# Gated cross-attention block on one core: rows scaled a batch further ahead, and a transfer that feeds float32r transposes

## The chip, the cores and the metric

The kernel runs on one core of a Trainium2 chip. The metric is the device time of one execution in microseconds (us). The kernel before was timed three times (median 298.14 us); one further execution, taken by the hardware profiler, took 297.72 us, and its span (first to last instruction) is 295.9 us. Durations below are of that execution. The engines are PE (TensorE, with its weight loads listed as PEld), ACT (ScalarE), DVE (VectorE), POOL (GpSimd) and SP (SyncE, which here only issues transfers).

## The reference, cut to what matters

```python
def _L0_xattn_ref(query, memories, mask, W, b):
    q = jnp.einsum('bsd,od->bso', query, W) + b
    add_mask = (1.0 - mask.astype(q.dtype)) * NEG
    attn_logits = jnp.einsum('bqd,bkd->bqk', q, memories) + add_mask
    attn_weights = jax.nn.softmax(attn_logits, axis=-1)
    return jnp.einsum('bqk,bkd->bqd', attn_weights, memories)

def _L0_ffn_ref(x, weight):
    return jnp.einsum('bsi,oi->bso', x, jnp.sign(weight))

x = x + jnp.tanh(g_xattn[0]) * _L0_xattn_ref(_layernorm(x), ctx, mask, W, b)
x = x + jnp.tanh(g_ffn[0]) * _L0_ffn_ref(_layernorm(x), weight)
```

`x` is 64 batches of 256 rows by 256 columns, `ctx` 64 batches of 77 keys by 256, all float32; `W` and `weight` are 256 by 256.

## The kernel before

A batch of 256 rows lies in SBUF as 128 partitions with two rows each (`j` = 0, 1). The work is software-pipelined over batches. In slot t every engine works in a fixed, hand-written order on several batches at once: PE transposes the probabilities of batch t-1 (`pt_ps`, L619), in even slots transposes the keys of two later batches (`ctx_ps`, L560), forms the logits of batch t (`l_ps`, L636) interleaved with the transposes of the attention result of batch t-2 (`x1t_ps`, L642), applies the probabilities of batch t-1 to the keys (`pv_ps`, L655), does half of a product of keys and query weights (`ctx_ps`, L568), transposes the scaled rows of batch t+1 (`xt_ps`, L601: four 128 by 128 transposes in float32) and last the feed-forward product of batch t-2 (`ffn_ps`, L673: eight matmuls of 256 columns in float32r, with the input split in a high part `x1_hi` and a low part `x1_lo`). An even slot and the odd one after it have different work, so times repeat in pairs of slots. `pipeline` runs slots 0 to 7 and 56 to 66 written out and slots 8 to 55 in a loop of eight.

The scaled rows `xs` are x times 1/deviation plus a shift, both found by DVE (`moments`, L437) and POOL (L270 to L286). ACT makes them (`scale_rows`, L333), one instruction for each j. ACT's order in slot t is: p_t (L395), in even slots ctx_t (L346), ffn_scaled (L402), xs of batch t+2 with j = 0, x_hi (L409), prob (L414), m_sb (L352), x_t of batch t+1 (`transposed_x`, L378), xs of batch t+2 with j = 1. `xs` has two buffers.

DVE's order is: the moments of x1, the reciprocal, y (L507), c1 (L518, which waits for the logits in `l_ps`), the masked logits and their extremes (L521), x_lo (L529), x1 (L537), the moments of x (L437). POOL's is: 1/deviation and shift of batch t+3, the second half of y (L313, which waits for ffn_scaled), the second 1/deviation, c2 (L324), neg_mask (L278).

SP issues, slot by slot: the load of x for batch t+5, in even slots the keys and masks of batches t+4 and t+5, and the store of y of batch t-3, which waits for DVE's and POOL's half of y. PE waits for `lo_done` (x_lo) before its feed-forward matmuls, for `xt_done` (x_t) before the logits, and for `pt_done` (p_t) before `pv_ps`.

Of the kernel before, what the change touches and what calls it, by code (L numbers as in the profile page):

```python
# [5 lines left out]
F32 = mybir.dt.float32  # L6
F32R = mybir.dt.float32r
I32 = mybir.dt.int32
ALU = mybir.AluOpType
ACT = mybir.ActivationFunctionType  # L10
AX = mybir.AxisListType

P = 128
N = 8
R = 4
# [5 lines left out]
DMA = 16  # L21


def flamingo_block(nc: bass.Bass, x: bass.AP, ctx: bass.AP, mask: bass.AP, g_xattn: bass.AP,
# [14 lines left out]
    NB, S, D = x.shape  # L39
    K = ctx.shape[1]  # L40
    T = S // P
# [8 lines left out]
    with ExitStack() as stack:  # L50
        def sb(name, shape, dt=F32):
            return stack.enter_context(nc.sbuf_tensor(name, shape, dt))

        def ps(name, shape):
            return stack.enter_context(nc.psum_tensor(name, shape, F32))

        def sem(name):
            return stack.enter_context(nc.semaphore(name))


        ident = sb("ident", [P, P])
        wq_raw = sb("wq_raw", [P, C, D])
        wq_c = sb("wq_c", [P, C, D])
        wf_raw = sb("wf_raw", [P, C, D])
# [16 lines left out]
        x_in = sb("x_in", [P, N, T, D])  # L81
# [1 line left out]
        ctx_v = sb("ctx_v", [K, N, D])  # L83
        ctx_t = sb("ctx_t", [P, C, 2, K])
        m_sb = sb("m_sb", [P, C, R, K])
        xs = sb("xs", [P, 2, T, D])
        x_t = sb("x_t", [P, 2, C, S])
        neg_mask = sb("neg_mask", [P, 2, T, K])
        neg_l = sb("neg_l", [P, 2, T, K])
# [22 lines left out]
        xt_ps = ps("xt_ps", [P, C, S])  # L112
# [11 lines left out]
        wf_loaded = sem("wf_loaded")  # L124
        ident_ready = sem("ident_ready")
        half_ready = sem("half_ready")
        gate_ready = sem("gate_ready")
        tanh_ready = sem("tanh_ready")
        prep_step = sem("prep_step")
# [11 lines left out]
        mr1_done = sem("mr1_done")  # L141
        shift1_done = sem("shift1_done")
        xs_done = sem("xs_done")
        negmask_done = sem("negmask_done")
        xt_psum = sem("xt_psum")
        xt_done = sem("xt_done")
# [26 lines left out]
        def at_least(eng, s, value):  # L173

            if not isinstance(value, int) or value > 0:
                eng.wait_ge(s, value)

        def landed(t0, n, ring=N):

            return t0 * (DMA // ring) + DMA * (n // ring + 1)  # L180

        def exists(t0, n):

            return not isinstance(t0, int) or 0 <= t0 + n < NB

        FIRST = N
        LAST = NB - N
        END = NB + 3

        def pipeline(eng, slot, after={}):  # L190

# [7 lines left out]
            with eng.Fori(FIRST // N, LAST // N) as group:  # L199
                for r in range(N):  # L200
                    slot(group * N, r)
            for t in range(LAST, END):
                slot(t - t % N, t % N)
# [4 lines left out]
        @block.sync  # L208
        def _(sp):
            def load_x(t0, n):  # L210
                sp.dma_start(x_in[:, n % N], x_rows[t0 + n]).then_inc(x_loaded[n % N], DMA)

            def load_mask(t0, n):

                i = n % N
                sp.dma_start(mask_in[:, i:i + 2],
                             mask_pairs[:, bass.ds(t0 + n, 2)]).then_inc(mask_loaded[i // 2], DMA)

            def load_ctx(t0, n):

                i = n % N
                sp.dma_start(ctx_v[:, i:i + 2],
                             ctx_keys[:, bass.ds(t0 + n, 2)]).then_inc(ctx_loaded[i // 2], DMA)

            load_x(0, 0)
            load_ctx(0, 0)
            load_x(0, 1)
            load_mask(0, 0)
            load_x(0, 2)
            load_ctx(0, 2)  # L230
            load_x(0, 3)
            load_mask(0, 2)
            load_x(0, 4)

            def slot(t0, r):
                t = t0 + r
                if exists(t0, r + AHEAD):
                    at_least(sp, x1_done, t - 2)
                    load_x(t0, r + AHEAD)
                if r % 2 == 0 and exists(t0, r + 4):  # L240
                    at_least(sp, pv_psum, t - 2)
                    at_least(sp, negmask_done, t - 2)
                    load_ctx(t0, r + 4)
                    load_mask(t0, r + 4)
                if exists(t0, r - 3):
                    i = (r - 3) % R
                    at_least(sp, y_done, t - 2)
                    at_least(sp, y_last_done, t - 2)
                    sp.dma_start(out_rows[t - 3], y[:, i]).then_inc(y_stored[i], DMA)

            pipeline(sp, slot)
            for i in range(R):
                sp.wait_ge(y_stored[i], DMA * (NB // R))
# [78 lines left out]
        def _(act):  # L332
            def scale_rows(t0, n, j):  # L333

                if j == 0:
                    act.wait_ge(shift1_done, t0 + n + 1)
                    act.wait_ge(x_loaded[n % N], landed(t0, n))
                    at_least(act, xt_psum, t0 + n - 1)
                act.activation(xs[:, n % 2, j], x_in[:, n % N, j], ACT.Identity,  # L339
                               scale=rstd1[:, n % R, j:j + 1],  # L340
                               bias=shift1[:, n % R, j:j + 1]).then_inc(xs_done, 1)

# [47 lines left out]
            def slot(t0, r):  # L390
                t = t0 + r
                if exists(t0, r - 1):
                    act.wait_ge(pt_psum, t)
                    at_least(act, pv_psum, t - 2)
                    act.activation(p_t[:, (r - 1) % 2], pt_ps[0:K, 0:S], ACT.Copy).then_inc(pt_done, 1)  # L395
                if r % 2 == 0 and exists(t0, r + 2):
                    keys_step(2 * t + 5)
                if exists(t0, r - 3):
                    act.wait_ge(c2_done, t - 2)
                    act.wait_ge(ffn_psum, t - 2)  # L400
                    at_least(act, y_last_done, t - 4)
                    act.activation(ffn_scaled[:, (r - 3) % 2], ffn_ps[T - 1][:, 0:D], ACT.Copy,  # L402
                                   scale=c2[:, (r - 3) % R, T - 1:T]).then_inc(ffn_scaled_done, 1)
                if exists(t0, r + 2):
                    scale_rows(t0, r + 2, 0)
                if exists(t0, r - 2):
                    act.wait_ge(x1t_psum, t - 1)
                    at_least(act, ffn_psum, t - 3)
                    act.activation(x1_hi[:, r % 2], x1t_ps[:], ACT.Copy).then_inc(hi_done, 1)  # L409
                if exists(t0, r):  # L410
                    act.wait_ge(logits_done, t + 1)
                    at_least(act, pt_psum, t - 1)
                    for j in range(T):
                        ins = act.activation(prob[:, r % 2, j], neg_l[:, r % 2, j], ACT.Exp, scale=-1.0,  # L414
                                             bias=neg_max[:, r % R, j:j + 1],
                                             accum_out=prob_sum[:, r % R, j:j + 1])
                    ins.then_inc(exp_done, 1)
                if isinstance(t, int) and t == 0:
                    gates()
                if r % 2 == 0 and exists(t0, r + 2):  # L420
                    m_step(0, (r // 2 + 1) % 2, 2 * t + 6)
                if r % 2 == 1 and exists(t0, r + 1):
                    m_step(1, (r // 2 + 1) % 2, 2 * t + 6)
                if exists(t0, r + 1):
                    transposed_x(t0, r + 1)
                if exists(t0, r + 2):
                    scale_rows(t0, r + 2, 1)

            pipeline(act, slot, {1: ffn_weights})


        @block.vector
        def _(dve):
            def moments(src, st, i, k, done):


                dve.bn_stats(st[:, k].rearrange("p j s -> p (j s)"),  # L437
                             src[:, i].rearrange("p j d -> p d j")).then_inc(done, 1)

            def stats1(n):  # L440
                dve.wait_ge(x_loaded[n], DMA)
# [18 lines left out]
            for c in range(C):  # L460
                ins = dve.tensor_scalar(wq_c[:, c], wq_raw[:, c], row_mean[:, c:c + 1], None, ALU.subtract)
# [91 lines left out]
        def _(pe):  # L553
# [10 lines left out]
            def m_step(c, count):  # L564

                pe.wait_ge(ctx_done, count)
                for o in range(C):
                    ins = pe.matmul(ctx_ps[:, 0:2 * K], wq_c[:, o, c * P:(c + 1) * P],  # L568
                                    ctx_t[:, o].rearrange("p b k -> p (b k)"),
                                    start=(o == 0), stop=(o == C - 1))  # L570
                ins.then_inc(ctx_psum, c + 1)
# [22 lines left out]

            def transpose_x(t0, n):

                pe.wait_ge(xs_done, T * (t0 + n + 1))
                at_least(pe, xt_done, t0 + n)
                for c in range(C):
                    for j in range(T):  # L600
                        ins = pe.transpose(xt_ps[:, c, j * P:(j + 1) * P],  # L601
                                           xs[:, n % 2, j, c * P:(c + 1) * P], ident[:])
                ins.then_inc(xt_psum, 1)

            transpose_x(0, 0)
            m_step(1, 2)

            def pair_keys(t0, r):
                pe.wait_ge(ctx_loaded[(r + 2) % N // 2], landed(t0, r + 2))
# [91 lines left out]
```

## Time and profile before

| | |
|---|---|
| three timed runs | 297.14, 298.14, 298.19 us |
| profiled execution | 297.72 us, span 295.9 us |
| PE / PEld busy | 285.6 / 275.4 us (97% / 93% of the span) |
| ACT, DVE, POOL busy | 253.9, 250.6, 214.1 us |
| granted TensorE clock, mean | 0.996 of full |
| moved by DMA | 44.39 MB, mean 150 GB/s |

A timeline row gives start, length and count of neighbouring equal instructions. PE's matmuls are pipelined: the length of one includes its latency, and what a matmul costs the stream is the distance from its start to the start of the next. Likewise on ACT an instruction may start shortly before the end of the one before it.

### The profile page before, as it was taken

The numbers are of one execution on the slowest core, as the hardware profiler recorded it, in microseconds if no ns is written. First come the engines' busy times: TensorE is split into PE (matmuls) and PEld (weight loads), VectorE is DVE, ScalarE is ACT, GpSimd is POOL, SyncE is SP. The second block draws the span as 40 slices with busy tenths as digits, with TensorE's granted clock in tenths as the row PEclk, the third lists the DMA queues.
The fourth block names the chain that finished last, engine by engine and source line by source line (L and its number), as shares of the span: only waits on it lengthen the run. The fifth ranks groups of instructions, "written<-read, shape, count | busy, mean of one in ns | idle before, by whom it ended". The sixth has DMA issues, their size and how long they took to land.

```text
span 295.9 us, 9253 instructions
## 1 busy us (share of the span) xinstructions
PE 285.6 (97%) x2338; PEld 275.4 (93%) x2338; DVE 250.6 (85%) x785; ACT 253.9 (86%) x738; POOL 214.1 (72%) x585
## 2 busy tenths in 40 slices
PE   7799999999999999999999999999999999999982
PEld 6599999999999999999999999999999999999972
DVE  3578988988898898889889888988988898898883
ACT  2689999999999998999999999999989999999841
POOL 2667777778777777877777787777778777777543
PEclk9999999999999999999999999999999999999998
DMA  6933445554544555454445545544654544441112
GB/s 192 281 90 115 149 143 154 188 167 145 161 153 142 159 184 168 137 167 154 141 156 184 171 140 160 153 143 155 184 172 138 167 151 143 154 151 71 73 56 88
DMA packets 33538, 44.39 MB, mean 150 GB/s; under 512 B 3504, under 2 KB 17136, under 8 KB 33520
## 3 DMA queue, kind: packets, MB, share of 16 engines
q1 hardware_dynamic: 32416, 43.66, 46.3%
q10 hardware_dynamic: 1104, 0.53, 0.6%
q8 instruction: 7, 0.11, 0.1%
q14 instruction: 11, 0.09, 0.1%
HBM read 27.40 MB, written 16.78 MB: 149 GB/s over the span
## 4 chain that ended last, share of the span: by engine, by line
PE 91%; DMA 3%; POOL 2%; DVE 1%; issue 1%; ACT 1%; SPq 1%; POOLq 0%; ACTq 0%
PE ffn_ps L673 20%; PE pv_ps L655 18%; PE l_ps L636 16%; PE ctx_ps L568 11%; PE x1t_ps L642 9%; PE xt_ps L601 9%; PE pt_ps L619 5%; PE ctx_ps L560 3%; DMA x_in<-in_x_dram 3%; POOL rstd L275 1%; POOL y L313 0%; DVE x_lo L529 0%; DVE c L518 0%; ACT ffn_scaled L402 0%; POOLq L50 0%
## 5 line engine op out<-in xcount | busy, mean ns | idle before, releaser
L275 POOL TENSOR_TENSOR rstd<-ve,minus_half 128x2 f32<-128x2 f32 x128 | 89.0, 695 | 10.0
L636 PE MATMUL l_ps<-m_sb,x_t 128*128 128x77 f32 x512 | 78.8, 257 | 0.9 <-ACT m_sb L352 0.5
L636 PEld LDWEIGHTS l_ps<-m_sb,x_t 128*128 128x128 f32 x512 | 74.6, 191 | 1.4 <-ACT x_t L378 1.3
L339 ACT ACTIVATE xs<-x_in,shift,rstd 128x256 f32<-128x256 f32 x126 | 74.6, 593 | 1.0 <-POOL shift L286 1.0
L642 PE MATMUL x1t_ps<-ident,x 128*128 128x128 f32 x256 | 68.8, 273 | 0.0
L655 PE MATMUL pv_ps<-ctx_v,p_t 77*128 77x256 f32 x256 | 66.1, 380 | 0.0
L673 PE MATMUL ffn_ps<-wf_t,x_hi 128*128 128x256 f32 x256 | 56.5, 301 | 2.5 <-DVE x_lo L529 2.4
L537 DVE SCALAR_TENSOR_TENSOR x<-pv_ps,c,x_in 128x256 f32<-128x256 f32 x128 | 55.3, 472 | 0.0
L414 ACT ACTIVATE prob<-neg_l,neg_max 128x77 f32<-128x77 f32 x128 | 44.6, 351 | 10.1 <-DVE neg_max L521 10.1
L313 POOL TENSOR_TENSOR y<-ffn_scaled,x 128x256 f32<-128x256 f32 x64 | 46.3, 724 | 9.2 <-ACT ffn_scaled L402 9.2
L529 DVE TENSOR_TENSOR x_lo<-x1t_ps,x_hi 128x512 fp32r<-128x512 f32 x64 | 43.9, 686 | 9.6 <-ACT x_hi L409 9.6
L673 PE MATMUL ffn_ps<-wf_t,x_lo 128*128 128x256 f32 x256 | 51.2, 282 | 0.0
L437 DVE BATCH_NORM_STATS2 st<-x_in 128x6 f32<-128x512 f32 x64 | 45.0, 704 | 6.9 <-DMA x_in<-in_x_dram 6.9
L270 POOL TENSOR_TENSOR ve<-st,eps 128x2 f32<-128x2 f32 x128 | 24.6, 192 | 33.9 <-DVE st L437 31.5
L642 PEld LDWEIGHTS x1t_ps<-ident,x 128*128 128x128 f32 x256 | 47.2, 185 | 0.0
L655 PEld LDWEIGHTS pv_ps<-ctx_v,p_t 77*128 77x128 f32 x256 | 43.5, 190 | 3.8 <-ACT p_t L395 0.3
L518 DVE TENSOR_TENSOR c<-recip,gate_attn 128x2 f32<-128x2 f32 x64 | 25.9, 405 | 23.2 <-PE l_ps L636 19.5
L568 PE MATMUL ctx_ps<-ctx_t,wq_c 128*128 128x154 f32 x256 | 44.4, 294 | 0.5 <-ACT ctx_t L346 0.5
L568 PEld LDWEIGHTS ctx_ps<-ctx_t,wq_c 128*128 128x128 f32 x256 | 41.0, 190 | 4.0 <-ACT ctx_t L346 0.7
L437 DVE BATCH_NORM_STATS2 st<-x 128x6 f32<-128x512 f32 x64 | 44.0, 688 | 0.2
L673 PEld LDWEIGHTS ffn_ps<-wf_t,x_hi 128*128 128x128 f32 x256 | 38.9, 189 | 4.0 <-DVE x_lo L529 3.8
L378 ACT ACTIVATE x_t<-xt_ps 128x512 f32<-128x512 f32 x64 | 38.3, 598 | 2.6 <-PE xt_ps L601 0.2
(49 smaller groups left out, 477.8 us busy)
## 6 DMA issues: line engine op xcount, KB each, us to landing
x_in<-in_x_dram SPq DMA_DIRECT2D x64, 256.0 KB, 2.7
out_dram<-y SPq DMA_DIRECT2D x64, 256.0 KB, 2.1
ctx_v<-in_ctx_dram SPq DMA_DIRECT2D x32, 154.0 KB
mask_in<-in_mask_BxSxS_ik_dram SPq DMA_DIRECT2D x32, 154.0 KB, 3.1
wq_raw<-in_L_xattn_W_dram ACTq DMA_DIRECT2D x1, 256.0 KB, 4.2
wf_raw<-in_L_ffn_weight_dram ACTq DMA_DIRECT2D x1, 256.0 KB, 5.6
bq_col<-in_L_xattn_b_dram ACTq DMA_DIRECT2D x1, 1.0 KB, 4.5
g_raw<-in_g_xattn_dram ACTq DMA_DIRECT2D x1, 0.5 KB, 6.2
```

The source lines that it names most:

```text
L275: pool.tensor_tensor(res[:, i], ve[:, i], minus_half[:], ALU.pow).then_inc(res_done, 1)
L313: pool.tensor_tensor(y[:, i, T - 1], ffn_scaled[:, (r - 3) % 2], x1[:, i, T - 1], ALU.add).then_inc(y_last_done, 1)
L339: act.activation(xs[:, n % 2, j], x_in[:, n % N, j], ACT.Identity, scale=rstd1[:, n % R, j:j + 1], bias=shift1[:, n % R, j:j + 1]).then_in ...
L414: ins = act.activation(prob[:, r % 2, j], neg_l[:, r % 2, j], ACT.Exp, scale=-1.0, bias=neg_max[:, r % R, j:j + 1], accum_out=prob_sum[:, ...
L437: dve.bn_stats(st[:, k].rearrange("p j s -> p (j s)"), src[:, i].rearrange("p j d -> p d j")).then_inc(done, 1)
L529: dve.tensor_tensor(x1_lo[:, r % 2], x1t_ps[:], x1_hi[:, r % 2].bitcast(F32), ALU.subtract).then_inc(lo_done, 1)
L537: ins = dve.scalar_tensor_tensor(out=x1[:, i, j], in0=pv_ps[:, j], scalar=c1[:, i, j:j + 1], in1=x_in[:, (r - 1) % N, j], op0=ALU.mult, op ...
L568: ins = pe.matmul(ctx_ps[:, 0:2 * K], wq_c[:, o, c * P:(c + 1) * P], ctx_t[:, o].rearrange("p b k -> p (b k)"), start=(o == 0), stop=(o == ...
L636: ins = pe.matmul(l_ps[:, j * K:(j + 1) * K], x_t[:, r % 2, c, j * P:(j + 1) * P], m_sb[:, c, r % R], start=(c == 0), stop=(c == C - 1))
L642: ins = pe.transpose(x1t_ps[:, c, j * P:(j + 1) * P], x1[:, (r - 2) % R, j, c * P:(c + 1) * P], ident[:])
L655: ins = pe.matmul(pv_ps[:, j], p_t[:, (r - 1) % 2, j * P:(j + 1) * P], ctx_v[:, i], start=True, stop=True)
L673: ins = pe.matmul(ffn_ps[j][:, 0:D], part[:, r % 2, c, j * P:(j + 1) * P], wf_t[:, c], start=(n == 0 and c == 0), stop=(n == 1 and c == C ...
```

## The change

Four things change. `xs` gets four buffers, and ACT makes both halves of a batch's scaled rows at the end of slot t, for batch t+3; only in slot 0 are those of batch 2 still made at the old places. For batches 4 to 59, SP issues at the head of slot t a transfer within SBUF, of 256 KB, that copies the scaled rows of batch t+2 into a new float32r tile `xs_r` with two buffers (through a view as float32, so the bits are kept); it waits for these rows. PE waits for this transfer in place of the rows and transposes from `xs_r` with a float32r identity, into a view of `xt_ps` as float32r. DVE makes that identity once, at its start. Batches 0 to 3 and 60 to 63 are transposed as before.

```diff
+        ident_r = sb("ident_r", [P, P], F32R)
-        xs = sb("xs", [P, 2, T, D])
+        xs = sb("xs", [P, R, T, D])
+        xs_r = sb("xs_r", [P, 2, T, D], F32R)
...
+        def moves(t0, n):
+            return not isinstance(t0, int) or MOVE_FIRST <= t0 + n < MOVE_END
+        def moved(t0, n):
+            return t0 * (DMA // 2) + DMA * ((n - MOVE_FIRST) // 2 + 1)
...
+        MOVE_FIRST = 4
+        MOVE_END = NB - 4
...
+            def move_xs(t0, n):
+                i = n % 2
+                sp.wait_ge(xs_done, T * (t0 + n + 1))
+                sp.dma_start(xs_r[:, i].bitcast(F32), xs[:, n % R]).then_inc(xs_moved[i], DMA)
             def slot(t0, r):
                 t = t0 + r
+                if moves(t0, r + 2):
+                    move_xs(t0, r + 2)
                 if exists(t0, r + AHEAD):
...
-                    at_least(act, xt_psum, t0 + n - 1)
-                act.activation(xs[:, n % 2, j], x_in[:, n % N, j], ACT.Identity,
+                    at_least(act, xt_psum, t0 + n - 3)
+                act.activation(xs[:, n % R, j], x_in[:, n % N, j], ACT.Identity,
...
-                if exists(t0, r + 2):
+                if isinstance(t, int) and t == 0:
                     scale_rows(t0, r + 2, 0)
...
-                if exists(t0, r + 2):
+                if isinstance(t, int) and t == 0:
                     scale_rows(t0, r + 2, 1)
+                if exists(t0, r + 3):
+                    for j in range(T):
+                        scale_rows(t0, r + 3, j)
...
+            dve.wait_ge(ident_ready, 2)
+            dve.tensor_copy(ident_r[:], ident[:]).then_inc(ident_r_ready, 1)
...
-                pe.wait_ge(xs_done, T * (t0 + n + 1))
+                if moves(t0, n):
+                    pe.wait_ge(xs_moved[n % 2], moved(t0, n))
+                else:
+                    pe.wait_ge(xs_done, T * (t0 + n + 1))
                 at_least(pe, xt_done, t0 + n)
                 for c in range(C):
                     for j in range(T):
-                        ins = pe.transpose(xt_ps[:, c, j * P:(j + 1) * P],
-                                           xs[:, n % 2, j, c * P:(c + 1) * P], ident[:])
+                        if moves(t0, n):
+                            ins = pe.transpose(xt_ps[:, c, j * P:(j + 1) * P].bitcast(F32R),
+                                               xs_r[:, n % 2, j, c * P:(c + 1) * P], ident_r[:])
+                        else:
+                            ins = pe.transpose(xt_ps[:, c, j * P:(j + 1) * P],
+                                               xs[:, n % R, j, c * P:(c + 1) * P], ident[:])
                 ins.then_inc(xt_psum, 1)
             transpose_x(0, 0)
             m_step(1, 2)
+            pe.wait_ge(ident_r_ready, 1)
```

## Rows read from the trace of the kernel before

**Rows 1.** The page: busy time by engine, and the last chain by line.

```profile
PE 285.6 (97%) x2338; PEld 275.4 (93%) x2338; DVE 250.6 (85%) x785; ACT 253.9 (86%) x738; POOL 214.1 (72%) x585
...
PE ffn_ps L673 20%; PE pv_ps L655 18%; PE l_ps L636 16%; PE ctx_ps L568 11%; PE x1t_ps L642 9%; PE xt_ps L601 9%; PE pt_ps L619 5%; PE ctx_ps L560 3%; DMA x_in<-in_x_dram 3%; POOL rstd L275 1%; POOL y L313 0%; DVE x_lo L529 0%; DVE c L518 0%; ACT ffn_scaled L402 0%; POOLq L50 0%
```

**Rows 2.** Waits from 24 to 278 us: last row (total, times, longest, us).

```profile
ACT p_t L395 <- PE pt_ps L619: 1.0, 6, 0.2
```

**Rows 3.** Timeline of PE: even slot from 156.57, one row of an odd slot.

```profile
153.79 1.03 PE L655 MATMUL pv_ps<-ctx_v,p_t 77*128 77x256 f32 x4
...
156.33 0.40 PE L673 MATMUL ffn_ps<-wf_t,x_lo 128*128 128x256 f32 x2
156.57 0.38 PE L619 MATMUL pt_ps<-ident,prob 128*77 128x128 f32 x2
156.79 0.43 PE L560 MATMUL ctx_ps<-ident,ctx_v 77*128 77x77 f32 x4
157.06 0.39 PE L636 MATMUL l_ps<-m_sb,x_t 128*128 128x77 f32 x2
...
157.97 0.34 PE L636 MATMUL l_ps<-m_sb,x_t 128*128 128x77 f32 x2
158.15 0.27 PE L642 MATMUL x1t_ps<-ident,x 128*128 128x128 f32 x1
158.26 1.03 PE L655 MATMUL pv_ps<-ctx_v,p_t 77*128 77x256 f32 x4
159.12 0.69 PE L568 MATMUL ctx_ps<-ctx_t,wq_c 128*128 128x154 f32 x4
159.65 0.60 PE L601 MATMUL xt_ps<-ident,xs 128*128 128x128 f32 x4
```

**Rows 4.** Timeline of ACT, two slots: their x_t and what follows.

```profile
151.65 0.60 ACT L378 ACTIVATE x_t<-xt_ps 128x512 f32<-128x512 f32 x1
...
155.82 0.60 ACT L378 ACTIVATE x_t<-xt_ps 128x512 f32<-128x512 f32 x1
156.32 0.59 ACT L339 ACTIVATE xs<-x_in,shift,rstd 128x256 f32<-128x256 f32 x1
156.99 0.38 ACT L395 ACTIVATE p_t<-pt_ps 77x256 f32<-77x256 f32 x1
157.27 0.42 ACT L346 ACTIVATE ctx_t<-ctx_ps 128x308 f32<-128x308 f32 x1
157.58 0.47 ACT L402 ACTIVATE ffn_scaled<-ffn_ps,c 128x256 f32<-128x256 f32 x1
157.94 0.60 ACT L339 ACTIVATE xs<-x_in,shift,rstd 128x256 f32<-128x256 f32 x1
158.46 0.60 ACT L409 ACTIVATE x_hi<-x1t_ps 128x512 fp32r<-128x512 f32 x1
```

**Rows 5.** Timeline of DVE and POOL, odd slot's c, then the even slot.

```profile
153.89 0.16 DVE L518 TENSOR_TENSOR c<-recip,gate_attn 128x2 f32<-128x2 f32 x1
...
158.26 0.72 POOL L313 TENSOR_TENSOR y<-ffn_scaled,x 128x256 f32<-128x256 f32 x1
158.35 0.65 DVE L518 TENSOR_TENSOR c<-recip,gate_attn 128x2 f32<-128x2 f32 x1 [0.58 <-PE l_ps L636]
...
159.24 0.68 DVE L529 TENSOR_TENSOR x_lo<-x1t_ps,x_hi 128x512 fp32r<-128x512 f32 x1
```

**Rows 6.** Timeline of SP's queue; the page's DMA queue and issues.

```profile
155.74 0.33 SPq L211 DMA_DIRECT2D x_in<-in_x_dram  x1
...
q1 hardware_dynamic: 32416, 43.66, 46.3%
...
x_in<-in_x_dram SPq DMA_DIRECT2D x64, 256.0 KB, 2.7
```

**Rows 7.** Timeline of the fill: ACT, POOL and PE.

```profile
14.02 0.65 POOL L286 TENSOR_TENSOR shift<-one,mr 128x2 f32<-128x2 f32 x1
...
14.67 0.59 ACT L339 ACTIVATE xs<-x_in,shift,rstd 128x256 f32<-128x256 f32 x1
15.16 0.37 ACT L395 ACTIVATE p_t<-pt_ps 77x256 f32<-77x256 f32 x1
...
15.77 1.07 PE L655 MATMUL pv_ps<-ctx_v,p_t 77*128 77x256 f32 x4
```

More of the change, by code:

```diff
@@ L126, in flamingo_block @@
         half_ready = sem("half_ready")
+        ident_r_ready = sem("ident_r_ready")
         gate_ready = sem("gate_ready")
@@ L143, in flamingo_block @@
         xs_done = sem("xs_done")
+        xs_moved = [sem(f"xs_moved{i}") for i in range(2)]
         negmask_done = sem("negmask_done")
```

## The prediction

> **What bounds the kernel now.** First the page. PE is busy for 97% of the span, and the chain that ended last runs through PE's lines almost alone [rows 1]; the transposes that the change touches, xt_ps, are 9% of it. Next the waits of the steady part: no row has PE or PEld as the waiting engine, and the last of all rows is 1.0 us in total [rows 2]. So PE's own stream sets the pace. The distance between two pv_ps, 153.79 and 158.26, is 4.47 us [rows 3], that between two x_t, 151.65 and 155.82, is 4.17 us [rows 4]: the first holds the even slot's key transposes, the second doesn't, and the even slot runs from 156.57 to about 161.04. A time that is taken from that stream is gained, as long as the other engines' answers are in time.
>
> **The price of a transpose.** Per instruction the stream costs the distance between starts [rows 3]. Float32: the four pv_ps take from 158.26 to 159.12, 0.215 us each for 256 columns, 0.84 ns a column. The four xt_ps take (0.60-0.27)/3 = 0.109 us each for 128 columns, 0.85 ns a column, so they run at the float32 rate. Float32r: the two ffn_ps from 156.33 to 156.57 take 0.12 us each for 256 columns, 0.46 ns a column. No row has float32r with fewer than 256 columns, nor a float32r transpose, so its price has to be bounded. From below: 128 columns at 0.46 ns are 0.059 us, and the nearest row for a weight load of 128 columns is ctx_ps at 156.79, four in 0.27 us, 0.067 us each. From above: two l_ps and one x1t_ps start within 157.97 to 158.15; the first step is some 0.07 us, like the 77 columns of ctx_ps, so the second is 0.11 us although only 77 columns stream in it. There the load of x1, or the turn to a transpose, is the limit. A float32r pass is 0.12 us at worst like ffn_ps. Between 0.059 (everything at the float32r rate) and 0.109 (nothing gained) I take the middle, 0.084 us: the operand is still four bytes wide to load and to pass through, only the stream is known to be faster.
>
> So four transposes a batch save 4 x 0.025 = 0.10 us, and 56 batches (4 to 59) save **5.6 us**. With 0.067 it would be 4 x 0.042 x 56 = 9.4 us, with 0.12 a loss of 2.5 us.
>
> The Trainium skill, "TensorE: Matmul & The Clock Gate", section "LDWEIGHTS (loading the stationary operand)", has a rule against this change: a load takes its columns divided by 1.2 GHz, whatever the rows. By it 128 columns would take 107 ns and hide any faster stream. The four ctx_ps at 0.067 us have a stationary operand of 128 columns too, and do not agree; the 0.11 us before x1t_ps does.
>
> **Can the others follow?** Before ffn_ps PE waits for x_lo. In the even slot x_lo ends at 159.92 [rows 5], and the last xt_ps starts at 159.65+0.33 = 159.98 [rows 3], with the load of ffn_ps right behind: no room at all. What makes x_lo late is c, which waits for the logits until 158.35 and then takes 0.65 us where the odd slot's takes 0.16; it ends at 159.00, with POOL's y (158.26+0.72 = 158.98) [rows 5].
>
> The Trainium skill, "SBUF — State Buffer", says that VectorE with two SBUF inputs and GpSimd share a port pair as an exclusive lock, and that the loser waits for the whole instruction; the 0.65 against 0.16 us agrees.
>
> The change moves that y. ACT's order after x_t becomes xs, xs, p_t, ctx_t, ffn_scaled. By distances between starts [rows 4]: x_t 155.82, first xs at +0.50, second at +1.02 (157.94 to 158.46 is 0.52 for an xs), p_t at +1.54 = 157.36, ctx_t +0.28, ffn_scaled +0.31 = 157.95, end 158.42 instead of 158.05. POOL's y can begin only near 158.48. c begins at 158.35 and is done at 158.51, ahead of it. x_lo then waits for x_hi alone (158.46+0.60), runs 159.09 to 159.77 and gives PE 159.82 with the usual 0.05 us for a signal: 0.16 us of room against 0.10 that I need. In the odd slot the y of POOL does not meet c, and the room by the same chain is about as large. x_hi itself isn't late: ACT is free at 158.31 and x1t_ps ends at 158.42.
>
> p_t is the second answer. In the odd slot x_t starts at 151.65, so p_t starts at 153.19 and ends at 153.57, and pv_ps starts at 153.79 with its load some 0.1 us earlier. 0.1 us is left where there was 0.5; it hides the move at nothing, and if an xs took 0.1 us longer PE would wait in every odd slot. In the even slot p_t ends at 157.74 for 158.26. ctx_t isn't needed until 159.12.
>
> **The transfer.** xs of batch t+3 ends in this trace at 155.82+1.02+0.59 = 157.43. SP now waits for it, in front of the load of x which stood at 155.74, so that load and the keys and masks behind it go some 2.1 us later; x lands in 2.7 us [rows 6], near 160.6, and DVE takes its moments at the end of the slot that begins at 161.04, behind an x_lo that comes 2.67 us into a slot (159.24 less 156.57), so after 163.7. The copy issued at 157.5 has no row of its own kind; at 2.7 us it lands at 160.2, and PE wants it in the slot from 161.04, as far into it as the odd slot's xt_ps lie: x_t at 155.82 starts as they end, 4.47+4.17 us before its counterpart of two slots on, so they start near 163.9. So over 3 us cover it, and 0 is the price. It adds 56 x 0.262 = 14.7 MB; 43.66 MB took 46.3% of the engines, so 62% will be busy: still no bound. The stores behind these issues wait for y anyway. DVE's copy of the identity falls in its first wait for x. Between 0 and +0.5 us for all of this.
>
> **The fill.** Here the change costs. In slot 0 ACT has to make two more xs in front of p_t. The second xs of batch 2 starts at 14.67, shift of batch 3 is there at 14.02+0.65 = 14.67, so p_t starts at 14.67+0.49+2 x 0.52 = 16.2 instead of 15.16 and ends at 16.57; pv_ps goes from 15.77 to about 16.65, **+0.9 us** [rows 7]. In slot 1 the same two xs and two copies of the ffn weights stand before p_t, some 0.3 us more, of which a wait for the first x_lo gives back a part. I take +1.0 us, between +0.4 and +1.5. The drain has no xs and doesn't change.
>
> **Sum.** 297.7 - 5.6 + 1.0 = 293.1 us for an execution like the profiled one. That lies 0.4 us below the median of the timed runs, so the forecast is **293.5 us**; own range 291 to 296.
>
> **Rivals.**
> (a) The full rate: 0.067 us or less. PE would save up to 0.17 us a slot, but x_lo allows 0.16: 298.1 + 1.0 - 56 x 0.16 = 290.1 us. For it speak ctx_ps's steps; against it, the 0.11 before x1t_ps. Chance 0.16.
> (b) The load of the four-byte operand is the bound, 0.11 us: nothing saved, the fill is lost, 299.2 us with 0 to +2.5 more. The Trainium skill's load rule leads here. Chance 0.15, mostly within the error.
> (c) float32r in short streams costs what a full float32 matmul costs, which is two instructions of 0.84 ns a column: 0.215 us for 128 columns. +0.106 x 4 x 56 = +23.7 us, 323 us. Only the absence of any float32r below 256 columns speaks for it; the kernel does its 154-column product in float32. Chance 0.08.
> (d) Slower by order: POOL's y begins before c in the even slot. Then c is held until 158.48+0.72 = 159.20, x_lo ends 0.20 later than now and PE's ffn_ps start 0.19 late, in 28 even slots: +5.3 us, while only 28 odd slots save 0.10. 298.1+1.0+5.3-2.8 = 301.6 us. It decides at 0.1 us: whether ffn_scaled ends before the logits do. A late p_t in odd slots would have the same sign. Chance 0.08.
> (e) The copy or the later loads aren't in time and PE waits for DMA: no row comes nearer than 3 us. 298 to 302 us. Chance 0.03.
> Forecast: 0.50.
>
> **How the numbers follow.** A difference of 0.5% (1.5 us) is what can be told from none. Faster: forecast and (a) together, 0.66. Slower by more: (c), (d), half of (e) and a third of (b): 0.21. The rest, 0.13, is no change. The range goes down to (a) with an easier fill, 289, and up past (b) to 300.5; outside are (c), most of (d) and a little below: some 0.17.
>
> **What would show it.** Right: four xt_ps some 0.52 us long in place of 0.60, no wait of PE in the steady part, distances between pv_ps of 4.37 us; c in even slots back at 0.16 us; pv_ps of the fill near 16.6. Wrong: steps of 0.11 or 0.2 us within xt_ps; PEld waiting for x_lo or p_t; c still at 0.65.

## The result and the profile after

| | before | changed |
|---|---|---|
| median of 20 timed runs | 297.94 us | 295.23 us |
| profiled execution, span | 297.72, 295.9 us | 296.76, 295.0 us |
| medians of a second series | 297.53 us (30 runs) | 296.82 us (12 runs) |

The ratio of the changed kernel to the one before is 0.9928, with an interval of 0.9914 to 0.9942: faster by 0.7%. In the second series it is 0.9971 (0.9947 to 0.9995). The sign was forecast, and the size was not: 1.5% was expected. One execution of each kernel (472.8 and 551.8 us) was in a much slower state and is left out of the ratio and of the spreads that follow. The changed kernel also spreads more, from 294.6 to 297.8 us in its first 20 runs (297.1 to 298.6 before), and part of the answer lies in that.

The page of the changed kernel, the lines on engines, the DMA queue and the new transfer:

```profile
PE 284.4 (96%) x2338; PEld 273.9 (93%) x2338; DVE 242.0 (82%) x786; ACT 250.9 (85%) x738; POOL 215.6 (73%) x585
...
q1 hardware_dynamic: 40480, 58.34, 60.7%
...
xs_r<-xs SPq DMA_DIRECT2D x56, 256.0 KB, 2.3
```

PE still bounds the kernel [rows 1]. The copies brought the queue from 46.3% to 60.7% [rows 6] and land in 2.3 us.

The waits of the steady part, 24 to 276 us, of the changed kernel:

```profile
POOL ve L293 <- DVE st L463: 20.9, 46, 2.7
DVE c L547 <- PE l_ps L674: 18.8, 46, 0.8
DVE x_lo L558 <- ACT x_hi L432: 14.2, 52, 0.3
ACT x_hi L432 <- PE x1t_ps L680: 10.9, 55, 0.3
```

PE is no waiting engine in any row of this view: neither the copy nor p_t makes it wait for long enough to show. Waits of some 0.1 us stay below what the view shows; those found below stand only in the distances between starts. ACT waits for x1t_ps, so it follows PE.

PE's timeline in a slot with key transposes, an ordinary one:

```profile
82.24 1.03 PE L693 MATMUL pv_ps<-ctx_v,p_t 77*128 77x256 f32 x4
83.11 0.69 PE L597 MATMUL ctx_ps<-ctx_t,wq_c 128*128 128x154 f32 x4
83.53 0.56 PE L634 MATMUL xt_ps<-ident_r,xs_r 128*128 128x128 f32 x4
83.93 0.47 PE L711 MATMUL ffn_ps<-wf_t,x_hi 128*128 128x256 f32 x2
84.23 0.40 PE L711 MATMUL ffn_ps<-wf_t,x_lo 128*128 128x256 f32 x2
```

The counterparts start at 158.26, 159.12 and 159.65 [rows 3]. From the start of the last of the four ctx_ps matmuls to that of the second ffn_ps the trace has 0.689 us before (159.523 to 160.212) and 0.613 after (83.503 to 84.116). So four transposes gave back 0.076 us in this slot. One steady pair of slots takes 8.62 us before (distances between pv_ps of 4.467 and 4.153) and 8.48 after (4.393 and 4.08 to 4.09).

Where the time of the two profiled executions went, by the starts of pv_ps in the two traces:

| stretch | before | changed | difference |
|---|---|---|---|
| start to the fourth pv_ps (fill) | 28.87 us | 30.97 us | +2.10 |
| fourth to the 62nd (steady part) | 249.80 us | 246.74 us | -3.06 |
| from there to the end of the span | 17.3 us | 17.3 us | 0.0 |

The -3.06 us consist of 28 pairs times 0.14 us, 3.9 us, of 0.2 us in seven distances that are 4.17 to 4.19 before where the others are 4.15, and of something that took 1.0 us back: seven of the distances after are 4.22 us, not 4.08 to 4.09. The rows of one of them, PE, DVE and POOL around 73.7 us, and below them DVE's and POOL's of the ordinary slot shown above. The xt_ps start 1.29 us after pv_ps here and in the ordinary slot, so what differs comes behind them:

```profile
73.55 0.20 POOL L309 TENSOR_TENSOR shift<-one,mr 128x2 f32<-128x2 f32 x1
73.62 1.03 PE L693 MATMUL pv_ps<-ctx_v,p_t 77*128 77x256 f32 x4
...
73.70 0.73 POOL L336 TENSOR_TENSOR y<-ffn_scaled,x 128x256 f32<-128x256 f32 x1
...
73.71 0.73 DVE L547 TENSOR_TENSOR c<-recip,gate_attn 128x2 f32<-128x2 f32 x1 [0.52 <-PE l_ps L674]
...
74.69 0.68 DVE L558 TENSOR_TENSOR x_lo<-x1t_ps,x_hi 128x512 fp32r<-128x512 f32 x1
...
74.91 0.56 PE L634 MATMUL xt_ps<-ident_r,xs_r 128*128 128x128 f32 x4
75.42 0.50 PE L711 MATMUL ffn_ps<-wf_t,x_hi 128*128 128x256 f32 x2
...
82.33 0.16 DVE L547 TENSOR_TENSOR c<-recip,gate_attn 128x2 f32<-128x2 f32 x1 [0.51 <-PE l_ps L674]
...
82.42 0.72 POOL L336 TENSOR_TENSOR y<-ffn_scaled,x 128x256 f32<-128x256 f32 x1
...
83.15 0.69 DVE L558 TENSOR_TENSOR x_lo<-x1t_ps,x_hi 128x512 fp32r<-128x512 f32 x1 [0.34 <-ACT x_hi L432]
```

At 73.7 POOL's y is 0.01 us ahead of DVE's c, c is held (that is, it lasts 0.73 us and ends with y, where it takes 0.16 alone), x_lo ends at 75.37, and ffn_ps starts 0.51 us after xt_ps where it is 0.40 in the ordinary slot. At 82.3 c is first and x_lo waits for x_hi only. It is rival (d) of the prediction, but in seven of 28 slots and at 0.13 to 0.14 us each. In 13 more of the 28 the two starts lie within 0.01 us of each other and c is not held.

ACT's rows of the same slot as at 73.7 say how the margin of 0.13 us between c and y went:

```profile
71.11 0.60 ACT L401 ACTIVATE x_t<-xt_ps 128x512 f32<-128x512 f32 x1
71.61 1.08 ACT L362 ACTIVATE xs<-x_in,shift,rstd 128x256 f32<-128x256 f32 x2
72.59 0.36 ACT L418 ACTIVATE p_t<-pt_ps 77x256 f32<-77x256 f32 x1
...
73.16 0.46 ACT L425 ACTIVATE ffn_scaled<-ffn_ps,c 128x256 f32<-128x256 f32 x1
```

From x_t to ffn_scaled it is 2.05 us where 2.13 were worked out (an xs costs 0.49 us to the next start, not 0.52), and from x_t to c it is 2.60 where [rows 4, 5] have 2.53. 0.08 on one side and 0.07 on the other are the whole margin.

ffn_scaled is not the only thing in front of y. In the kernel before it ended at 158.05, 0.21 us before y began; the row in front of y there is POOL's own:

```profile
158.12 0.20 POOL L286 TENSOR_TENSOR shift<-one,mr 128x2 f32<-128x2 f32 x1
```

y began 0.14 us after the start of shift before, and 0.15 after it at 73.7, where ffn_scaled had ended 0.08 us earlier (73.62). In sched_only, with shift long done, it also begins 0.08 us after the end of ffn_scaled. So in the changed kernel both are ready within 0.01 us, and the later ffn_scaled moves y, against a kernel in which shift alone decides, by hardly more than that.

### The profile page after: what moved, and what is told of

It is laid out like the page before. It is cut to its first block, busy times and chain, and to the rows that moved or that the text cites. A ratio compares the mean times of both kernels' runs of the same rounds, so it can differ in the third digit from the quotient of the medians.

```text
span 295.0 us, 9382 instructions
## 1 busy us (share of the span) xinstructions
PE 284.4 (96%) x2338; PEld 273.9 (93%) x2338; DVE 242.0 (82%) x786; ACT 250.9 (85%) x738; POOL 215.6 (73%) x585
## 3 DMA queue, kind: packets, MB, share of 16 engines
q1 hardware_dynamic: 40480, 58.34, 60.7%
## 4 chain that ended last, share of the span: by engine, by line
PE 90%; DMA 3%; POOL 2%; ACT 2%; DVE 1%; issue 1%; SPq 1%; POOLq 0%; ACTq 0%
PE ffn_ps L711 22%; PE pv_ps L693 18%; PE l_ps L674 16%; PE ctx_ps L597 11%; PE x1t_ps L680 9%; PE xt_ps L634 6%; PE pt_ps L657 5%; PE ctx_ps L589 3%; DMA x_in<-in_x_dram 3%; PE xt_ps L637 1%; POOL rstd L298 1%; ACT xs L362 1%; POOL y L336 0%; DVE x_lo L558 0%; DVE c L547 0%
## 5 line engine op out<-in xcount | busy, mean ns | idle before, releaser
L362 ACT ACTIVATE xs<-x_in,shift,rstd 128x256 f32<-128x256 f32 x126 | 68.1, 590 | 0.6 <-POOL shift L309 0.5
L336 POOL TENSOR_TENSOR y<-ffn_scaled,x 128x256 f32<-128x256 f32 x64 | 46.9, 732 | 9.6 <-ACT ffn_scaled L425 9.2
L432 ACT ACTIVATE x_hi<-x1t_ps 128x512 fp32r<-128x512 f32 x64 | 38.2, 597 | 12.4 <-PE x1t_ps L680 12.1
L597 PE MATMUL ctx_ps<-ctx_t,wq_c 128*128 128x154 f32 x256 | 45.1, 298 | 0.5 <-ACT ctx_t L369 0.5
L597 PEld LDWEIGHTS ctx_ps<-ctx_t,wq_c 128*128 128x128 f32 x256 | 41.7, 193 | 4.0 <-ACT ctx_t L369 0.7
L711 PEld LDWEIGHTS ffn_ps<-wf_t,x_lo 128*128 128x128 f32 x256 | 39.3, 188 | 0.0
```

The costliest lines, as they stand in the source:

```text
L336: pool.tensor_tensor(y[:, i, T - 1], ffn_scaled[:, (r - 3) % 2], x1[:, i, T - 1], ALU.add).then_inc(y_last_done, 1)
L362: act.activation(xs[:, n % R, j], x_in[:, n % N, j], ACT.Identity, scale=rstd1[:, n % R, j:j + 1], bias=shift1[:, n % R, j:j + 1]).then_in ...
L711: ins = pe.matmul(ffn_ps[j][:, 0:D], part[:, r % 2, c, j * P:(j + 1) * P], wf_t[:, c], start=(n == 0 and c == 0), stop=(n == 1 and c == C ...
```

## The experiments

Kernels of one series ran on the same chip and share the runs of the kernel before; each series had another chip. Series A (before 297.53 us): sched_only, after_again, fill_spread, c_one_input. Series B (before 297.50 us): y_after_c, both, copy_unused, direct_r. Series C (before 298.20 us): the last three. Ratios are to the kernel before within the series, with the interval.

| kernel | median us | ratio | pv_ps distances, us | c held |
|---|---|---|---|---|
| sched_only | 298.62 | 1.0031 (1.0011 to 1.0052) | 4.47, 4.16 | 0 |
| after_again | 296.82 | 0.9971 (0.9947 to 0.9995) | 4.39, 4.09, some 4.23 | 7 |
| fill_spread | 295.32 | 0.9923 (0.9893 to 0.9952) | 4.39, 4.09, some 4.23 | 4 |
| c_one_input | 298.30 | 1.0011 (0.9991 to 1.0032) | 4.39, mostly 4.23 | 21 |
| y_after_c | 294.10 | 0.9884 (0.986 to 0.9908) | 4.39, 4.08 | 0 |
| both | 293.31 | 0.9863 (0.9836 to 0.989) | 4.39, 4.08 | 0 |
| copy_unused | 299.18 | 1.0053 (1.0035 to 1.0071) | 4.47, 4.15 | 0 |
| direct_r | 297.10 | 0.9994 (0.9972 to 1.0016) | 4.39, mostly 4.22 | 23 |
| direct_r_y_after_c | 293.87 | 0.9852 (0.9824 to 0.988) | 4.39, 4.08 | 0 |
| before_y_after_c | 297.70 | 0.9989 (0.9974 to 1.0003) | 4.47, 4.15 | 0 |
| both_twice | 312.25 (one run) | | 4.73, 4.43 | 0 |

"c held" counts instances of DVE's c above 0.7 us in the steady part of the profiled execution; the kernel before has 0.65 to 0.70 us in each slot with key transposes, so it was held there too, by a y that began 0.04 to 0.09 us earlier.

### The order alone

```diff
-                if moves(t0, r + 2):
-                    move_xs(t0, r + 2)
...
-                            ins = pe.transpose(xt_ps[...].bitcast(F32R), xs_r[...], ident_r[:])
+                        ins = pe.transpose(xt_ps[...], xs[:, n % R, j, ...], ident[:])
```

> Only the new order on ACT and the four buffers of xs; no copy, all transposes in float32 from xs. Theory (the transposes are the only gain, the fill is a cost): the steady distances between pv_ps stay at 4.15 and 4.47 us, since PE's stream is unchanged; the fill costs about 1 us or, if PE's clock falls there, 2; so 0.2 to 0.8% slower than before. POOL's y against DVE's c in the slots with key transposes: c is held (0.65 to 0.73 us) in only a part of them, and PE does not notice because its own stream leaves room. Rival (the order on ACT itself gains, since x_lo came late before): 0.5% or more faster than before without any float32r.

Measured: 0.3% slower; the steady distances are those of before to 0.01 us, 4.472 and 4.161. Its fourth pv_ps is at 29.35, 0.5 us later than before. The order frees c in every slot, where a part had been expected (y begins at least 0.05 us after c), and that alone is worth nothing. The rival falls.

### The changed kernel once more

> The changed kernel unchanged, a second profile. Theory: steady distances 4.39 and 4.09 us again; the number of slots in which c is held varies between executions or stays near 7 of 28, each costing about 0.13 us; the fill either has the drop to half clock (second pv_ps near 22.4 us, span about 295) or not (second pv_ps near 20.9, span about 293.4), which would explain why 20 executions spread from 294.6 to 297.1. Rival (the copy makes the spread): the distances themselves would differ from the first profile or PE would show waits for the copy.

Measured: the profiled execution took 295.48 us with a span of 293.7. Steady distances as in the first profile, again seven held c. What differs is the fill. First after_again, then the changed kernel's first profile: the first pv_ps, and the windows (us, busy time and count of PE, PEld, DVE, ACT, POOL, granted clock, DMA share, GB/s):

```profile
16.47 1.13 PE L693 MATMUL pv_ps<-ctx_v,p_t 77*128 77x256 f32 x4 [0.62 <-ACT p_t L418]
...
18.00:20.00 2.00, 2.00 (x22) 2.00 (x21) 1.80 (x5) 1.78 (x5) 0.64 (x2) 1.00 0.03 8
20.00:22.00 2.00, 1.66 (x12) 1.36 (x11) 0.68 (x6) 2.00 (x8) 1.60 (x6) 1.00 0.32 117
```

```profile
16.71 1.13 PE L693 MATMUL pv_ps<-ctx_v,p_t 77*128 77x256 f32 x4 [0.62 <-ACT p_t L418]
...
18.00:20.00 2.00, 2.00 (x10) 1.97 (x10) 2.00 (x5) 1.20 (x6) 0.41 (x2) 0.50 0.00 0
20.00:22.00 2.00, 2.00 (x17) 2.00 (x16) 0.03 (x1) 2.00 (x7) 1.70 (x5) 0.69 0.04 8
```

PE stands still for 0.62 us before this pv_ps in both, waiting for p_t. In after_again the clock stays at full (2.4 GHz), in the first profile it falls to 0.50 (1.2 GHz) from 18 to 20 us, and the second pv_ps is at 22.42 instead of 21.03. In the kernel before, the clock was full there. Over all the profiled executions: six have this stop of 0.62 us before the first pv_ps (the changed kernel twice, sched_only, c_one_input, y_after_c, copy_unused), and in three of them the clock fell; in the seven without it, it never did. In sched_only and copy_unused the stops of PE from 13 to 17 us are the same to 0.01 us (0.31 and 0.63), and it fell in one of the two only. The fill costs 0.8 us (fourth pv_ps at 29.68 for 28.87) without the fall and 2.1 with it.

The other executions have no trace, but each has its mean granted clock. In the 13 profiled ones it is 0.993 or less with the fall in the fill and 0.994 or more without (it also counts the fall at the end of the kernel, which all have). Of 19 executions of the changed kernel in the first series, seven have 0.993 or less, with a median of 296.8 us, and the other twelve have a median of 295.2. In the second series it is six of twelve, 297.5 against 296.2. Of the 30 executions of the kernel before in that series one has it. So the clock goes with 1.4 to 1.6 us of the spread within a series. The stop of 0.62 us isn't needed for a low mean: direct_r has no such stop in its profile, and two of nine of its executions have 0.985 and take 298.8 and 299.0 us, where its other seven have a median of 297.0.

### The lead gained more slowly

```diff
-                if isinstance(t, int) and t == 0:
-                    scale_rows(t0, r + 2, 0)
+                first = isinstance(t, int) and t < 3
+                if first:
+                    for j in ((0,), (0, 1), (1,))[t]:
+                        scale_rows(t0, r + 2, j)
...
-                if exists(t0, r + 3):
+                if first and t == 1:
+                    scale_rows(t0, r + 3, 0)
+                if exists(t0, r + 3) and not (first and t < 2):
```

> The changed kernel, but the batch of lead is gained over slots 1 and 2 instead of in slot 0: both halves of batch 3 where ACT waits for the extremes in slot 1, the first half of batch 4 at the end of slot 1 and its second half in slot 2 after p_t. Theory (the fill costs 1 us by p_t and up to 1.5 more by the clock): the first pv_ps is back near 15.8 us, the second near 20.0, the granted clock stays 1.0 from 14 to 24 us; total 1 to 2 us (0.3 to 0.7%) under the changed kernel. Rival (the fill's delay is absorbed later or comes from the copies): the same time as the changed kernel.

Measured: 0.9923 against 0.9971 of after_again in the same series; the intervals just overlap, the medians are 1.5 us apart. The first pv_ps is at 15.57 us, PE no longer waits for p_t, and the clock is full in the fill. But the second is at 20.73, not 20.0: there PE waits 0.72 us for the probabilities, whose DVE work stands behind the preparation of the ffn weights, and that starts at 14.25 us in this execution. In `both`, the same fill, it starts at 13.17 and the second pv_ps is at 19.64; over all the profiled executions it starts between 12.64 and 14.25, whatever the kernel. Not all of the 1.5 us is the fill: the two profiled executions differ by 0.5 us in span, 0.4 of it in the steady part, where four c are held and not seven. The rest of the 1.5 goes in part with the clock, which is at 0.993 or less in one execution of seven here and in six of twelve there; among the others the medians are 295.2 and 296.2.

### c with one tensor in SBUF

```diff
-                    dve.tensor_tensor(c1[:, i], recip[:, i], gate_attn[:], ALU.mult).then_inc(c1_done, 1)
+                    dve.tensor_scalar(c1[:, i], recip[:, i], gate_attn[:, 0:1], None, ALU.mult).then_inc(c1_done, 1)
```

> The changed kernel, but DVE makes c1 with gate_attn as a per-partition scalar, so the instruction has one tensor in SBUF instead of two. Theory (c is held by POOL's y because both want a second read from SBUF; where it is held PE's ffn_ps waits for x_lo): c takes about 0.16 us in all slots and no distance of 4.22 us is left, total about 1 us (0.3%) under the changed kernel. Rival (any small DVE instruction that starts within POOL's y is held, or the 4.22 distances have another cause): held instances stay, time the same.

Measured: the opposite, 298.30 us. One line of its c, of the profile's view by source line (ns shortest, median, longest), and the same of y_after_c:

```profile
L547 DVE TENSOR_SCALAR c<-recip,gate_attn x64: 228/229/765, 16.7 to 287.0; 128x2 f32<-128x2 f32 x64
```

```profile
L549 DVE TENSOR_TENSOR c<-recip,gate_attn x64: 148/160/286, 16.8 to 282.5; 128x2 f32<-128x2 f32 x64
```

A tensor_scalar is held as well, up to 0.765 us, and more often: in five of the 21 it had begun 0.015 us before y and was held all the same. My reason, the second tensor, is wrong as the only condition. The price is confirmed the hard way: with 21 held c instead of 7, most of the distances in slots with key transposes are 4.23 us, and the steady part takes 248.90 us against 246.74. This profiled execution also has the fall of the clock in the fill (second pv_ps at 22.15), and eight of the twelve executions have a mean clock of 0.993 or less.

### POOL's y behind c

```diff
                     pool.wait_ge(ffn_scaled_done, t - 2)
+                    if exists(t0, r - 1):
+                        pool.wait_ge(c1_done, t)
```

> The changed kernel, but POOL's y also waits for DVE's c of the same slot, so that it can't begin first. Theory (c is held for as long as POOL's y runs, whatever kind of small DVE instruction it is, and where it is held PE's ffn_ps comes 0.13 us late): c is 0.16 us in every slot but the last two, no distance of 4.22 us is left, 7 x 0.13 = 0.9 us (0.3%) under the changed kernel, which gave 293.7 us of span with a fill at full clock. Rival (the long distances come from the loop or from transfers): they stay.

Measured: c is 0.16 us at the median and 0.29 at most (the line above) and no long distance is left. 294.10 us, 0.9884, where after_again had 0.9971. By the medians this is 2.7 us, between two series; by the two profiled executions, both at full clock in the fill, it is 1.4 us (spans 293.7 and 292.3): the steady part, without the seven held c, is 1.06 us shorter (245.68 for 246.74) and the fill 0.3. The rest of the 2.7 us is not explained by this edit.

### Both edits

> The changed kernel with the lead gained over slots 1 and 2 and with POOL's y behind c. Theory: both gains add: the granted clock stays full in the fill, all steady distances are 4.39 and 4.09 us, span near 292.2 us, time near 294 us, 1.2% under before. Rival (they overlap or the wait on POOL costs something): not under fill_spread's 294.95 us.

Measured: 293.31 us, ratio 0.9863, span 291.4; pv_ps of the fill at 15.42 and 19.64, the fourth at 28.47, 0.4 us before that of the kernel before. The changed kernel without its two side effects is 1.4% faster. All five executions have a mean clock of 0.994 or more.

### The copy, unused

```diff
-                            ins = pe.transpose(xt_ps[...].bitcast(F32R), xs_r[...], ident_r[:])
+                        ins = pe.transpose(xt_ps[...], xs[:, n % R, j, ...], ident[:])
```

PE still waits for the copy.

> The changed kernel with order, buffers and copy, PE waits for the copy, but all transposes are in float32 from xs. Theory (the copy and the later loads are hidden): the same as with the order alone, distances 4.16 and 4.47 us, PE never waits for the copy, 298.5 us. Rival (the 256 KB copies cost PE something, by contention or by late loads of x): slower than the order alone by over 0.3%.

Measured: distances of 4.466 and 4.154 us, those of the kernel before, and PE waits for nothing in the steady part. There the 14.7 MB of copies are hidden. In the profiled execution what lies over before is the fill, with the clock at 0.51 from 18 to 20 us (fourth pv_ps at 30.62). That doesn't explain the median: seven of the ten executions have a mean clock of 0.994 or more, and theirs is 299.1, where those of sched_only have 298.5 in a series with the same time before. By whole times up to 0.6 us for the copy is not excluded; the rival asked for over 0.3% and is not met (1.0053 against 1.0031).

### float32r without lead and copy

```diff
-        xs = sb("xs", [P, 2, T, D])
+        xs = sb("xs", [P, 2, T, D], F32R)
...
-                        ins = pe.transpose(xt_ps[:, c, j * P:(j + 1) * P],
-                                           xs[:, n % 2, j, c * P:(c + 1) * P], ident[:])
+                        ins = pe.transpose(xt_ps[:, c, j * P:(j + 1) * P].bitcast(F32R),
+                                           xs[:, n % 2, j, c * P:(c + 1) * P], ident_r[:])
```

> The kernel before, with its order and its two buffers, but ACT writes xs as float32r itself and all 64 batches are transposed in float32r; no copy. The scaled rows are rounded by that, so the logits are of lower precision. Theory (in the kernel before c is held in each slot with key transposes and x_lo leaves PE no room there): only the other slots gain their 0.07 us, distances about 4.45 and 4.09 us, some 32 x 0.07 = 2.2 us (0.7%) faster, DVE's c still 0.65 us in every second slot, and PE waits for x_lo there. Rival (the transposes gain in every slot whatever c does): 64 x 0.07 = 4.5 us, 1.5% faster.

Measured: not even that, 0.9994. One distance of a pair falls to 4.39 and the other rises to 4.22, which is 8.61 us against 8.62 for the pair. DVE's c and POOL's y of this kernel, with what stands before y on ACT and POOL:

```profile
71.88 0.73 DVE L523 TENSOR_TENSOR c<-recip,gate_attn 128x2 f32<-128x2 f32 x1 [0.52 <-PE l_ps L642]
```

```profile
71.11 0.47 ACT L404 ACTIVATE ffn_scaled<-ffn_ps,c 128x256 f32<-128x256 f32 x1
...
71.71 0.20 POOL L288 TENSOR_TENSOR shift<-one,mr 128x2 f32<-128x2 f32 x1
71.86 0.73 POOL L315 TENSOR_TENSOR y<-ffn_scaled,x 128x256 f32<-128x256 f32 x1
```

y is first again, c is held in 23 of the 29 steady slots with key transposes, and what PE saves in two slots it waits for in one. The view of waits has no row of PE here either. y begins 0.15 us after the start of shift and 0.28 after the end of ffn_scaled: without the new order POOL's own row decides when it begins. Cheaper transposes alone are worth nothing in this kernel.

### The same with POOL's y behind c

> The kernel before with ACT writing xs as float32r (the rows are rounded by that) and all 64 batches transposed in float32r, no copy and no lead, and POOL's y behind DVE's c. Theory (what the direct form gave in one slot it lost to the held c in the next): c is 0.16 us in all steady slots, distances 4.39 and 4.08 us, 62 slots x 0.07 = 4.3 us under before, about 293.3 us (1.4%). Rival (without the lead x_lo is late anyway, or p_t is): PE still waits in some slots and less than 0.7% is gained.

Measured: 293.87 us, 0.9852, as fast as `both`, with no copy, no lead and two buffers; 4.39 and 4.08 us in all slots and one slot more than the changed kernel has at either end. Its price is that the scaled rows are written as float32r; what that does to the result was not measured.

### The wait alone, in the kernel before

> The kernel before with only POOL's y behind DVE's c; float32 transposes. Theory (in the kernel before the held c costs nothing because PE's own stream is as long): distances stay 4.47 and 4.15 us with c at 0.16 us, time within 0.2% of before. Rival (the held c costs time before as well, and part of the gain has nothing to do with float32r): over 0.5% faster.

Measured: 0.9989 (0.9974 to 1.0003). c is 0.16 us in each slot (0.19 at most) and nothing is gained. The held c cost nothing as long as PE's stream was as long as the chain through x_lo; it costs once PE is faster. The fill of this execution, with the old order and a full clock, has its fourth pv_ps at 29.53, 0.7 us later than the kernel before: so much the fill varies by itself.

### The transposes twice

```diff
-                for c in range(C):
+                for c in [c for c in range(C) for _ in range(2 if moves(t0, n) else 1)]:
```

> The best version so far, with each of the four float32r transposes of batches 4 to 59 issued twice. Theory (a float32r transpose of 128 columns costs 0.084 us in a row of its kind, the rest of the 0.36 us of four is paid once at the turn to or from float32): the steady distances grow by 4 x 0.084 = 0.34 us at most, and steps within xt_ps are 0.084. Rival (each costs 0.09): by 0.36 us. Below 0.34, a part of the added time would lie where PE has to wait for x_lo anyway, and there is none in this version.

```profile
153.30 0.91 PE L640 MATMUL xt_ps<-ident_r,xs_r 128*128 128x128 f32 x8
```

Measured, in one execution: the distances are 4.734 and 4.433 us, 0.341 and 0.353 more than in `both`: 0.085 to 0.088 us for each added transpose, nearer the theory (0.34) than the rival (0.36). In the first four the saving against float32 was only 0.076 us instead of 4 x 0.024 = 0.10, so about 0.02 us are paid once per slot around the float32r transposes. What they are paid for isn't shown: the number of turns between float32 and float32r is the same before and after, only the turn now stands in front of xt_ps and not of ffn_ps.

## Why the prediction was right or wrong

- **PE's stream as the bound: right**, but for seven waits of 0.13 to 0.14 us behind held c. The views of waits have no row of PE before or after, and don't show these.
- **Price of one float32r transpose, 0.084 us: right, and in part luck.** The doubled kernel adds 0.085 to 0.088 each, but 0.084 was only the middle between two bounds, and no row pointed at it. The Trainium skill's load rule ("TensorE: Matmul & The Clock Gate", "LDWEIGHTS (loading the stationary operand)") would have it at 0.107 at least; the runs do not agree.
- **The term 5.6 us: this term failed, it measured 3.9.** I multiplied a step by four. A slot saves 0.067 to 0.076 us, not 0.10, since some 0.02 us are paid once around these four; the prediction put that at nothing, without a reason. Loss of the forecast: 1.7 us.
- **"c begins at 158.35 and is done at 158.51, ahead of it": this step failed.** The two starts were 0.13 us apart in the estimate, and the estimate had an error of 0.15. In the profile it is a matter of 0.01 us which comes first, and seven of 28 slots fell on the wrong side. The estimate also looked at ffn_scaled alone and left out POOL's own shift, right behind which y began before the change. Cost 7 x 0.14 = 1.0 us, shown by y_after_c, where it is gone and the steady part is 1.06 us shorter. That it was seven and not 23 as in direct_r is luck, by 0.01 us or so. Rival (d) had the mechanism right and at 0.19 us each in all 28 slots it was too dear; I should have given it as a share of slots within the forecast, not as a case of its own.
- **The cause of the hold: wider than I took it.** c_one_input shows a tensor_scalar, with one tensor in SBUF, held too, for 0.74 to 0.77 us. The Trainium skill, "SBUF — State Buffer", section "Who interferes with whom", names a second tensor in SBUF as one condition. The page also has VectorE's two-port modes contend, and says that tensor_scalar can enter them; the hold in c_one_input would fit that, but no trace here shows the mode.
- **x_lo's room: right, and more important than I took it.** direct_r shows a saving on PE that x_lo takes back in full. With the new order the transposes pay (7 held c, where direct_r has 23), and the rows put that down to the later ffn_scaled and y; the order alone gains nothing (sched_only). Since direct_r lacks the copy as well, the order's part is argued. What is shown is that y behind c is enough: direct_r_y_after_c is at 0.9852 without order and copy.
- **p_t, the copy, later loads: right in the steady part.** No wait; copy 2.3 us for 2.7 taken; queue at 60.7% for 62%.
- **The fill: the mechanism was right, and the first pv_ps is late as forecast** (15.87 to 16.71, mean 16.26, in six executions with the new order, and mean 15.39 in the four with the old one: +0.87 for +0.9). By the fourth pv_ps less is left at full clock: 29.35 to 29.68 in three executions against 28.84 to 29.53 in four, +0.3 by the means, so +1.0 was too much there. What I left out is that PE can fall to half clock there: the fourth pv_ps is then at 30.62 to 30.97, +2.1 us in the profiled execution.

The sum for the profiled pair: -3.9 - 0.2 (seven steps of 0.01 to 0.03 us, which before has and after has not) + 1.0 for the held c + 2.1 = -1.0 us, measured -1.0. Forecast for it was -4.6. By the medians of the first series, where most executions kept the clock, it is -2.7. One sum of the prediction is off by a little: its terms for "slower by more" add up to 0.225, not 0.21. `both` and direct_r_y_after_c show that 293.3 to 293.9 us was there to be had, with both side effects gone.

What stays open: which property of a small DVE instruction makes POOL's y hold it; what the 0.02 us around the float32r transposes are; and why the medians of the changed kernel differ by 1.6 us between the two series (and chips) while those of the kernel before differ by 0.4. The clock explains only a part: executions at 0.994 or more differ by 1.0 us between the series too (295.2 and 296.2), and those at 0.993 or less by 0.8. How many c were held in them only a trace would tell.

## What to carry to other kernels

Before an engine's stream is shortened, write down by how much the next answer it waits for is early; where that is zero, as it was in every second slot here, the gain can be zero until that chain is shortened too, as in direct_r. Where the order of two instructions that exclude each other is left to chance by 0.1 us, let a semaphore decide it: the wait cost nothing, and with it the changed kernel reached 1.2% where it had 0.3 to 0.7% without. Extra work in front of a critical answer in the fill can cost double if TensorE's clock drops: here 2.1 us with the drop and 0.8 without. Look at the mean clock of every execution, not only of the profiled one. And a view of waits is blind to waits of 0.1 us; distances between starts are not.

## What the runs showed of the hardware

- A float32r transpose of 128 by 128 took 0.085 us in a row of its kind, a float32 one 0.109 us, at the full clock.
- A copy of 256 KB within SBUF took 2.3 us from issue to landing, with 14.7 MB of them beside 44 MB of other traffic; with them and float32 transposes (copy_unused) PE's steady distances stayed at 4.466 and 4.154 us.
- A DVE tensor_tensor on two columns (0.16 us alone) took 0.72 to 0.74 us when POOL's 256-column y began up to 0.03 us before it, and ended with it; with y 0.04 to 0.09 us ahead it took 0.65 to 0.70. Begun before y it took 0.16; with y less than 0.006 us ahead both were seen. As a tensor_scalar (0.23 alone) it took 0.74 to 0.77 us, also where it had begun up to 0.016 us before y, and 0.23 when it had begun 0.06 or more before.
- After the same stops of PE from 13 to 17 us, the granted clock from 18 to 20 us was 1.00 in sched_only and 0.51 in copy_unused.
